# Pairwise feature products: four adjacent output rows per partition instead of two, with a different batch in each half of the weight columns

## The reference

```python
# r_feature: (2048, 200, 64), L0_rec_weight: (200, 64, 64)
bilinear = jnp.einsum('bie,ied->bid', feature, weight)
out = jnp.einsum('bid,bjd->bij', bilinear, feature)   # (2048, 200, 200)
```

## Time and profile before

| | |
|---|---|
| median of 3 runs | 1304.34 us (1304.11 to 1307.31) |
| the profiled execution, its own time | 1306.27 us |
| its span, first to last instruction | 1304.5 us |
| busy: PE, PEld (weight loads) | 1198.4 us (92%), 1030.4 us (79%) |
| busy: ACT, DVE, POOL | 1056.7 us (81%), 925.6 us (71%), 247.1 us (19%) |
| DMA, mean of the span | 337 GB/s |
| granted TensorE clock, mean | 0.987 |

### The profile page before, as it was taken

How to read it: one execution, slowest core, us unless ns; L and a number is a source line. 1 busy time by engine, 2 the same in 40 slices (tenths; PEclk the granted TensorE clock), 3 DMA queues, 4 the chain that set the end, 5 groups by cost and what they waited for, 6 DMA issues and landing times.

```text
span 1304.5 us, 56312 instructions
## 1 busy us (share of the span) xinstructions
PE 1198.4 (92%) x24384; PEld 1030.4 (79%) x24384; DVE 925.6 (71%) x1792; ACT 1056.7 (81%) x1185; POOL 247.1 (19%) x375
## 2 busy tenths in 40 slices
PE   5999999999989999999989989899998999889985
PEld 4788788887778878897778878788777887778864
DVE  0477677777777768677776777777766777677795
ACT  4898787987889877997879977799787987779964
POOL 2111111122211112111121211212121112111111
PEclk9999999999999999999999999999998999999998
DMA  9699999999999999999999999999999999999899
GB/s 243 208 354 358 335 339 345 356 348 363 325 349 347 357 347 344 345 354 351 347 351 337 335 325 347 357 354 330 360 351 316 347 325 345 322 341 347 311 345 318
DMA packets 266133, 439.58 MB, mean 337 GB/s; under 512 B 40608, under 2 KB 237216, under 8 KB 265888
## 3 DMA queue, kind: packets, MB, share of 16 engines
q1 hardware_dynamic: 222112, 317.90, 69.6%
q0 software_dynamic: 43776, 118.09, 28.4%
HBM read 108.13 MB, written 327.68 MB: 334 GB/s over the span
## 4 chain that ended last, share of the span: by engine, by line
PE 66%; DMA 14%; issue 6%; DVE 5%; ACT 5%; SPq 2%; ACTq 0%; POOLq 0%; DVEq 0%
PE ps L286 43%; DMA out_dram<-staging 12%; PE ps L255 12%; PE ps L268 11%; ACT staging L316 3%; DVE staging L316 2%; SPq L189 2%; DMA x<-feature_dram 2%; ACT bl L338 2%; DVE win L363 2%; DVE win L371 1%; DMA w<-weight_dram 1%; DVE win L370 1%; ACT xt L328 0%; SPq L179 0%
## 5 line engine op out<-in xcount | busy, mean ns | idle before, releaser
L286 PE MATMUL ps<-win,bl 64*64 64x200 f32 x16384 | 840.2, 339 | 60.1 <-ACT staging L316 35.3
L286 PEld LDWEIGHTS ps<-win,bl 64*64 64x64 f32 x16384 | 674.5, 175 | 152.4 <-issue 58.8
L316 ACT COPY staging<-ps 128x800 f32<-128x800 f32 x768 | 625.8, 868 | 164.9 <-PE ps L286 67.6
L316 DVE COPY staging<-ps 128x800 f32<-128x800 f32 x256 | 253.2, 989 | 207.8 <-PE ps L286 206.4
L363 DVE COPY win<-xt 128x400 f32<-128x400 f32 x512 | 282.9, 553 | 138.5 <-ACT xt L328 78.0
L338 ACT COPY bl<-ps 128x1024 f32<-128x1024 f32 (+1 forms) x208 | 305.1, 1467 | 36.8 <-PE ps L268 35.3
L231 POOL DMA_DIRECT2D out_dram<-staging x256 | 161.6, 631 | 890.5 <-DVE staging L316 541.9
L268 PE MATMUL ps<-xt,w 64*64 64x128 f32 x6400 | 235.8, 275 | 13.8 <-issue 12.0
L255 PE MATMUL ps<-ident,x 128*128 128x128 f32 x1600 | 224.3, 283 | 21.4 <-DMA x<-feature_dram 15.5
L328 ACT COPY xt<-ps 128x1024 f32<-128x1024 f32 (+1 forms) x208 | 212.1, 1020 | 36.6 <-PE ps L255 36.2
L255 PEld LDWEIGHTS ps<-ident,x 128*128 128x128 f32 x1600 | 175.1, 143 | 73.5 <-issue 65.5
(11 more groups left out here) (2 smaller groups left out, 0.2 us busy)
## 6 DMA issues: line engine op xcount, KB each, us to landing
out_dram<-staging SPq DMA_DIRECT2D x768, 400.0 KB, 6.3
x<-feature_dram POOLq DMA_DIRECT2D x96, 1024.0 KB, 8.9
out_dram<-staging POOLq DMA_DIRECT2D x256, 50.0 KB, 5.8
x<-feature_dram POOLq DMA_DIRECT2D x16, 256.0 KB, 5.8
w<-weight_dram SPq DMA_DIRECT2D x24, 128.0 KB, 6.8
w<-weight_dram SPq DMA_DIRECT2D x2, 64.0 KB, 6.2
```

Source lines behind the costliest of these rows:

```text
L286: last = nc.tensor.matmul(tile[64 * g:64 * g + 64, h ^ g, F * b:F * (b + 1)], lines_of_bl(n, h, g, R * ORDER[s // 2] + r), win[64 * h:64 * ...
L316: copy(staging[:, slot, PB * s % OCT:PB * s % OCT + PB].rearrange("p b h j -> p h b j"), tile_of("s", n, s)[:, :, 0:PB * F].rearrange("p h ...
```

## The change

Output rows are now dealt out four at a time. A quad is 4 adjacent output rows of one batch; there are 50, and two halves of 64 places hold them for two batches: PSUM partitions 0 to 63 belong to the first batch of a set, 64 to 127 to the second. So each partition's staged run is 800 numbers, 3200 bytes in a row in DRAM. For that a line becomes features 2m+1 and 2m+2 (the last line wraps to feature 199 and feature 0), the weights are loaded shifted by one in one half, and x is loaded from feature 1 on with a small extra load of feature 0 (L296).

- Stores: SP still issues three of 32 partitions for four sets, now 4 runs of 800 numbers each instead of 8 of 400; POOL issues two of 2 partitions instead of one of 4 (L313).
- x: one run of 2048 numbers a partition instead of two of 1024.
- Weighing: 17 groups (`NW`) a block instead of 13, each of three quads (12 products; one group of two quads has 8). A group's tile has four slots of 64 batches for each half and bank, one of which in each half is not written. `store_bl` copies all four with one instruction, 1024 numbers as before; group 14 takes two copies of 256 numbers, and the last takes three, of 384, 128 and 256. For odd n such a copy writes 4 neighbouring numbers at a time. Because unwritten slots are read, DVE sets the PSUM tiles to zero at the start (L464) and PE waits for that.
- Window: `fill_own` has one more copy, of 64 partitions by 4 numbers (L451).
- Order: the last transposes of a block now come behind set 51 (57 before); weighings come behind sets 6, 10, ... 58 and then 60, 61 and 62 (5 to 60 before).

```diff
-    out_v = out.rearrange("b (m h) j -> m b (h j)", h=2)
+    out_v = out.rearrange("(s g) (k r) j -> (g k) s (r j)", g=2, r=4)
...
-    transposed_at = {60 * u // NG + 2: u for u in range(NG)}
-    weighed_at = {s + 3: u for s, u in transposed_at.items()}
+    transposed_at = {56 * u // NG: u for u in range(NG)}
+    weighed_at = {sets_before(j) if j < NW - 3 else SETS - 1 - NW + j: j for j in range(NW)}
...
                 for z in range(3):
-                    sp.dma_start(out_v[Z * z:Z * (z + 1), b:b + OCT, :],
-                                 staging[z:128:4, slot].rearrange("p b h j -> p b (h j)")
+                    sp.dma_start(out_v[2 + z:2 + z + 3 * 31 + 1:3, OCT * q:OCT * q + OCT, :],
+                                 staging[z:128:4, slot].rearrange("p s r j -> p s (r j)")
                                  ).then_inc(out_written[slot], 16)
...
+                for g in range(2):
+                    nc.gpsimd.dma_start(out_v[98 * g:98 * g + 2, OCT * q:OCT * q + OCT, :],
+                                        staging[64 * g + SPARE[0]:64 * g + SPARE[1] + 1:4, slot
+                                                ].rearrange("p s r j -> p s (r j)")
+                                        ).then_inc(rest_written[slot], 16)
...
-                            last = nc.tensor.matmul(tile[64 * g:64 * g + 64, h ^ g, F * b:F * (b + 1)],
-                                                    lines_of_bl(n, h, g, R * ORDER[s // 2] + r),
-                                                    win[64 * h:64 * h + 64, q % WSLOTS, r, 1 - h:1 - h + F],
+                            last = nc.tensor.matmul(tile[64 * g:64 * g + 64, r, at:at + F],
+                                                    rows_of_bl(n, r, g, i, s),
+                                                    win[64 * r:64 * r + 64, q % WSLOTS, 2 * (s % 2) + g, 1 - r:1 - r + F],
...
-                at = "p g c v a -> p g c v a" if n % 2 == 0 else "p g c v a -> p v a g c"
-                weighed = bilinear_tile(n, u).rearrange("p g c (a v) -> p g c v a", a=4)
-                nc.scalar.copy(group_of_bl(n, u).rearrange(at), weighed.rearrange(at)).then_inc(bl_stored, 1)
+                if j == NW - 3:
+                    act.wait_ge(bl_stored, n * NW + j)
+                for piece in pieces(j):
+                    last = nc.scalar.copy(piece_of_bl(n, j, piece), piece_of_tile(n, j, piece))
+                last.then_inc(bl_stored, 1)
...
+                nc.vector.tensor_copy(win[64:128, slot, :, 0], quad_of_xt(n, k)[64:128, LINES - 1, C - 1, :])
```

More of the change, by code:

```diff
@@ L29, in feature_interaction @@
     NG = LINES // 2 + 1
+    NW = FH // 6 + 1
     NX = NG // 2 + 1
     QUADS = CELLS
-    PB = 2
-    SETS_B = NB // PB
+    SETS = NB // 2
     XSLOTS = 2
     TILES = 4
-    OCT = 8
+    OCT = 4
     OSLOTS = 3
     WSLOTS = 4
[L39 to L44, removed]
+    ROW = 4 * F
@@ new lines, in row_of, with line_of, quads_of, positions @@
+    def row_of(r, i):
+        return 2 * r + (i ^ r)
+    def line_of(f):
+        return (f - 1) % F // 2, (f + 1) % 2
+    def quads_of(j):
+        if j == NW - 3:
+            return [0, 1]
+        first = 3 * (j - (j >= NW - 3)) + 2
+        return [first, first + 1, first + 2]
+    def positions(g, k):
+        k -= 2 * (1 - g)
+        return 4 * (k // 3) + k % 3 if 0 <= k < 48 else SPARE[k % 48 if k >= 48 else k + 2]
+    def slots(g, j):
+        return [0, 2, 3] if g and j != NW - 3 else [0, 1, 2][:len(quads_of(j))]
@@ new lines, in sets_before @@
+    def sets_before(j):
+        return max(positions(g, k) for k in quads_of(j) for g in range(2)) + 1
+    transposed_at = {56 * u // NG: u for u in range(NG)}
+    weighed_at = {sets_before(j) if j < NW - 3 else SETS - 1 - NW + j: j for j in range(NW)}
+    assert len(transposed_at) == NG and len(weighed_at) == NW and max(weighed_at) < SETS
+    assert list(weighed_at) == sorted(weighed_at)
+    assert all(s + 1 >= sets_before(j) for s, j in weighed_at.items())
+    assert all(sum(t < s for t in transposed_at) >= transposed_for(j) for s, j in weighed_at.items())
@@ L68, in feature_interaction @@
+    fillings = []
+    for j in range(NW):
+        fillings += [("t", 0, u) for u in transposed_before(j)] + [("b", 0, j)]
     for n in range(BLOCKS):
[L69 removed]
+        for s in range(SETS):
             fillings.append(("s", n, s))
@@ L138, in quad_of_xt, with steps_of_bl, piece_of_bl, piece_of_tile @@
             return xt[:, 0:LINES, k, :, :] if n % 2 == 0 else xt[:, k, 0:LINES, :, :]
[L140 to L150, removed]
+        def steps_of_bl(n):
+            return (NB, 1) if n % 2 == 0 else (1, NB)
+        def piece_of_bl(n, j, piece):
+            g, halves, slot, quads = piece
+            line, batch = steps_of_bl(n)
+            at = [dict(zip(slots(gg, j), (positions(gg, k) for k in quads_of(j)))) for gg in range(2)]
+            pos = at[g][slot]
+            step = at[g][slots(g, j)[-1]] - at[g][slots(g, j)[-2]] if quads > 1 else 1
+            for gg in range(g, g + halves):
+                for k, p in at[gg].items():
+                    assert not slot <= k < slot + quads or p == at[gg][slot] + step * (k - slot)
+            first = bl[:, 0, 0]
+            i = [64 * line, 2]
+            half = [64 * batch + (at[1][slot] - pos) * line if halves > 1 else 1, halves]
+            quad = [step * line, quads]
+            sets = [batch, SETS]
+            return bass.AP(first.tensor, first.offset + pos * line + 64 * g * batch,
+                           [first.ap[0]] + ([i, half, quad, sets] if n % 2 == 0 else [half, sets, i, quad]))
+        def piece_of_tile(n, j, piece):
+            g, halves, slot, quads = piece
+            weighed = bilinear_tile(n, j)[:, :, g:g + halves, slot:slot + quads, :]
+            return weighed if n % 2 == 0 else weighed.rearrange("p i g k s -> p g s i k")
+        def rows_of_bl(n, r, g, i, s):
+            half = slice(64 * r, 64 * r + 64)
+            places = slice(64 * i, 64 * i + 64)
+            at = 64 * g + s
             return bl[half, places, at] if n % 2 == 0 else bl[half, at, places]
```

199 lines of the change are left out of this document (106 added, 93 removed).

## The result

The changed kernel takes 1363.8 us (median of 4, 1359.1 to 1377.3) against 1305.8 us for the kernel before: a ratio of 1.0458 (interval 1.0393 to 1.0523). It is slower by 58 us where the forecast was faster by 22, and it lies outside the range. The profiled execution took 1377.25 us, the longest of its kernel, with a span of 1375.5, 71.0 us more than before.

A forecast was written before the change was run, and what follows sets the result against it. The DMA engines were taken as the bound, PE 4.5 us a block behind. Savings of 18 us over 15 blocks and 4.8 in the last, together 23, less 1 at the start, gave 1284 us profiled, 1282 median; range 1254 to 1330.

The forecast's parts named there:

- Stores: SP's output stores: 3200-byte runs save 12.4 ns on each of 98,304 pairs, 76 us over 16 engines, 4.8 us a block.
- Copies on ACT: Weighing copies into `bl`: about 1.1 us each in odd blocks, ACT busy 63.5 us odd and 64.5 even, nothing credited.
- The first rival: Odd-layout weighing copies stay slow at 2.02 us, ACT paces odd blocks: about 1321 us, up to 1335; chance 0.17.
- PE for the work of a block, and its wait for `bl`: PE stays busy 74.4 us a block and waits 1.0 us at each block's end, about 15 us in all.
- The block's term: Each of 15 blocks: 74.4 us PE work, 1.0 block-end wait, 2.3 remaining idle, 77.7 us; 1.2 saved, 18 in all.
- x, "I take nothing": Loads of x: at most 10 us of DMA time saved by longer runs, 2.8 us given back by extra loads; none credited.
- POOL, "Nothing": POOL's queue: 272 more issues cost 180 us, a third of the span in all, x loads two slots ahead; nothing charged.
- The last block: Final block, without transposes or weighing: falls by the stores' 4.8 us to 66.7 us, with DVE's busy time below that.
- a last block near 71 us: Sign of a wrong forecast: a final block still taking 71 us would mean the stores did not get cheaper.
- "Slower": Outcome of a slower kernel: chance 0.29, from 0.17 for slow odd copies and 0.12 for stores priced by bytes alone.
- The second one: Rival: stores cost by bytes alone, DMA keeps 78.9 us a block; 1321 us at worst, 1296 with partial saving; chance 0.25.
- the new wait at the end of a block: PE's wait for ACT's last weighing copies before the next block's first set: 0.7 to 2 us, taken as 1.0.

## Why the prediction was wrong, step by step

- **Stores: right.** From 51 to 1306 us q1 moved this, beside q0:

```profile
q1 hardware_dynamic: 103227, 293.68, 60.7%
q0 software_dynamic: 37061, 108.60, 28.5%
```

  60.7% of 16 engines over 1255 us for 293.68 MB is 41.5 us of one engine a MB; the earlier trace rows give 45.1. For 327.68 MB over 16 engines that saves 75 us, where the text took 76. The two kernels without loads (the one before the change first), from 100 to 1100 us, give 44.9 and 42.3 us a MB, which saves 53 us, so that the match with 76 is partly luck:

```profile
q1 hardware_dynamic: 182198, 274.41, 77.0%
...
q1 hardware_dynamic: 96241, 273.81, 72.4%
```

  By the Trainium skill's rule (DMA: Bandwidth & Descriptors, "Why small descriptors are slow") the estimate was 25 us; both measurements decide against it here. q0 gave some back: 52.7 in place of 50.0 us a MB, 18 us over the loads.
- **Copies on ACT: right.** The 240 full `bl` copies take 1066 ns in the mean of both layouts, 1.1 us was taken; ACT is busy 66.1 us in an odd and 63.8 in an even block (63.5 and 64.5 forecast). The first rival is out. The odd copies alone (51 to 134.4 us), then the groups of the whole span:

```profile
L423 ACT COPY bl<-ps 128x1024 f32<-128x1024 f32 x15 | 16.1, 1076 | 0.0
...
L423 ACT COPY bl<-ps 128x1024 f32<-128x1024 f32 x240 | 255.5, 1066 | 14.3 <-PE ps L355 14.2
...
L451 DVE COPY win<-xt 64x4 f32<-64x4 f32 x512 | 95.7, 187 | 86.5 <-ACT xt L411 41.6 <-PE ps L372 29.7
```

- **PE for the work of a block, and its wait for `bl`: right.** 75.3 us a block on the mean, 74.4 forecast, and 16.4 us in all for the wait, 15 forecast.
- **The block's term: here it failed.** It gave 77.7 us as PE's work, 1.0 us at the block's end and "the half of today's 4.5 us idle that I do not charge to landing stores". It took for granted that stores which need less DMA time land in time for ACT. The median store of SP did land a little sooner, 5.9 us from issue in place of 6.3:

```profile
out_dram<-staging SPq DMA_DIRECT2D x768, 400.0 KB, 6.3
...
out_dram<-staging SPq DMA_DIRECT2D x768, 400.0 KB, 5.9
```

  But the stores that ACT waits for are those beside the loads, and the term counted what the new order puts on ACT and PE at a block's end, not the loads that move with the transposes: two of 1 MB at sets 47 and 51, beside which a store took 11.2 us, then sets 52 to 63 without a transpose, then three weighings that wait behind the blocked ACT, then a DMA that runs empty. ACT's wait for landing stores doubled where it was to halve, from 47 to 104 us. The order of the weighings was never varied alone, so its share in this is argued from the timeline. 83.6 - 77.7 = 5.9 us, over 15 blocks 89 of the 93 us by which the profiled execution missed its 1284 us.
- **x, "I take nothing", and POOL, "Nothing": wrong with it.** The packets' count was priced, not what a load does to the stores beside it. Runs of 4 KB instead of 8 are worth about 14 us, smaller loads 17, loads apart 19, transposes spread 18. Together that is 69 of the 82 us by which the median missed 1282, in the order in which these steps were taken.
- **The last block: wrong for another reason.** 66.7 us was forecast by its stores, 69.8 came. DVE was set aside by its busy time (56.7 + 3.8 us), though it works there as a chain of 2 x (0.187 + 0.566 + 0.383 + 0.381) + 0.988 = 4.0 us for four sets, 64 us for sixteen, and the start and the drain come on top. So a last block near 71 us, named as the sign of stores that did not get cheaper, nearly came for a reason of its own: with less work on DVE the block took 64.4 us, below the forecast. The copy priced at 0.12 us takes 187 ns; the earlier trace rows have no row of its shape.
- **The rivals.** "Slower" had the sign and a chance of 0.29, but for other mechanisms; neither reached 1364. That two nearly full resources may both lose when the order between them changes was no rival at all. The second one, in which "the new wait at the end of a block comes on top", was nearest in form, but its wait is the one for `bl`, and the stores did get cheaper.
- **A reading of the rows.** The 332 to 340 GB/s with loads are those of the blocks shown in the earlier trace rows; over all 15 blocks the trace has 330 to 350, so they do not set the loads apart from the 347 of the last block.

The Trainium skill (DMA: Bandwidth & Descriptors, "Queues, rings and completion order") says that each DMA engine takes turns between its queues, a packet at a time; a packet is there a group of descriptors, typically 9 to 17, and not one of the profile's packets. The stretch at 201.5 us, with 1.16 MB on q0 beside 0.79 MB on q1, fits such turns. Why runs of 8 KB cost the stores more than runs of 4 KB does not follow from it, and no run here shows it.

## What to carry to other kernels

Before crediting saved DMA time to a stage, list in order what each queue issues there, loads too, and ask for each slot how long its stores take with those loads beside them, against the time until the engine comes back to it. When work is moved between stages, the loads tied to it move too: keep them small and evenly apart, and keep the last sets of a block as dense as the others. An engine on a chain is judged by the chain's time for one round, not by its busy share.

## What the runs showed that was not expected

- Loads of the same bytes with the same runs, 512 KB apart instead of in pairs, are worth 19 us of 1332.
- Without loads both kernels run at 1198 us with PE 96% busy; of the 108 us that the loads add to the kernel before, 47 stand in PE's busy time (1151.2 to 1198.4 us), though it does the same products.
- The mean granted clock of the span fell from 0.987 to 0.970. It does not follow the stalls block by block: among the changed kernel's blocks one of 83 us has 0.96 and one of 86 us has 1.00.
- A copy of 4 numbers in 64 partitions takes DVE 187 ns.
